# A state-space scan whose preparation moves into its own loop, with work shifted from VectorE to GpSimd and one transpose moved in the attention

## The reference, cut to what matters

```python
A = -jnp.exp(A_log)                                   # 512 x 16
xp = jnp.einsum('bld,rd->blr', x, x_proj_w)           # 48 rows: dt_in, B, C
dt = jax.nn.softplus(jnp.einsum('blr,dr->bld', dt_in, dt_proj_w) + dt_proj_b)
dA = jnp.exp(dt[..., None] * A)
dBx = dt[..., None] * B[:, :, None, :] * x[..., None]
def step(h, inp):                                     # over the 512 tokens
    dA_t, dBx_t, C_t = inp
    h = dA_t * h + dBx_t
    y = jnp.einsum('bdn,bn->bd', h, C_t)
    return (h, y)
y = jnp.moveaxis(ys, 0, 1) + D * x
```

## Time and profile before

| | us |
|---|---|
| median of 3 runs | 2287.24 |
| lowest, highest | 2269.8, 2289.48 |
| profiled execution, its own time | 2282.19 |
| its span, first to last instruction | 2280.4 |

### The profile page before, as it was taken

One profiled execution on the slowest core, in us unless ns is written; L12 is line 12 of the kernel. 1 busy time (PEld: TensorE's weight loads), 2 busy tenths in 40 slices (PEclk: granted clock), 3 DMA queues, 4 the chain that ended last, 5 costly groups with the idle time before them and its releaser, 6 DMA issues. The chain is left out here.

```text
span 2280.4 us, 27810 instructions
## 1 busy us (share of the span) xinstructions
PE 1827.1 (80%) x8232; PEld 1115.2 (49%) x8232; DVE 1625.2 (71%) x2905; ACT 804.5 (35%) x1301; POOL 736.5 (32%) x582
## 2 busy tenths in 40 slices
PE   6287778787758899936986888888873999999998
PEld 1022222222436888825862333333452777877786
DVE  4699999999634566665207888888458766667668
ACT  5243434343211444421213666666523111111112
POOL 2676767674250566654001000000011422112100
PEclk7599999999779898857996999999985999999999
DMA  8011111111030888753544333333000000000002
GB/s 300 23 42 38 37 37 37 37 37 32 13 148 6 280 282 277 247 166 134 193 187 112 85 91 88 84 94 80 3 30 28 28 28 28 1 28 28 1 1 74
DMA packets 102032, 197.64 MB, mean 87 GB/s; under 512 B 17257, under 2 KB 34025, under 8 KB 101019
## 3 DMA queue, kind: packets, MB, share of 16 engines
q1 hardware_dynamic: 96795, 179.46, 24.2%
q0 software_dynamic: 5120, 16.78, 2.2%
HBM read 130.72 MB, written 63.05 MB: 85 GB/s over the span
## 5 line engine op out<-in xcount | busy, mean ns | idle before, releaser
L1527 DVE TENSOR_REDUCE att_top<-att_first 128x1 f32<-128x512 f32 x512 | 332.4, 686 | 121.6 <-PE att_first L1407 111.6
L421 PE MATMUL scan_y<-scan_hc,all_ident 128*128 128x512 f32 x512 | 294.7, 663 | 101.8 <-DVE scan_hc L381 101.7
L355 POOL TENSOR_TENSOR scan_dbx<-ssm_U,scan_bbc 128x512 f32<-128x512 f32 x256 | 316.0, 1268 | 135.1 <-DVE scan_h L390 101.4
L390 DVE TENSOR_TENSOR_SCAN scan_h<-scan_da,scan_dbx 128x512 f32<-128x512 f32 x256 | 318.3, 1244 | 23.0 <-POOL scan_dbx L355 22.1
L1489 ACT ACTIVATE att_prob<-att_second 128x1024 f32<-128x1024 f32 x256 | 247.9, 1022 | 132.6 <-PE att_second L1427 130.6
L366 ACT ACTIVATE scan_da<-ssm_DT,ssm_A 128x512 f32 x256 | 176.8, 691 | 270.9 <-DVE scan_h L390 270.9
L421 PEld LDWEIGHTS scan_y<-scan_hc,all_ident 128*128 128x128 f32 x512 | 79.1, 194 | 314.0 <-DVE scan_hc L381 312.5
L1673 POOL TENSOR_TENSOR pairs_raw<-pairs_raw,pairs_scales 128x512 f32<-128x512 f32 x42 | 42.6, 1048 | 547.5 <-DMA pairs_raw<-in_w 547.5
L1803 ACT ACTIVATE ffn_silu<-ffn_pg 128x256 f32<-128x256 f32 x112 | 43.2, 386 | 415.2 <-PE ffn_pg L130 415.2
L128 PE MATMUL ffn_pg<-pairs_wh,last_XH 128*128 128x512 f32 x448 | 180.4, 403 | 1.7 <-PEq L431 1.7
L1407 PE MATMUL att_first<-att_ks,att_qs 48*128 48x512 f32 x512 | 133.8, 513 | 59.5 <-DVE att_top L1527 48.5
(11 more groups left out here) (272 smaller groups left out, 3913.7 us busy)
## 6 DMA issues: line engine op xcount, KB each, us to landing
mlps_raw<-in_w SPq DMA_DIRECT2D x26, 769.0 KB, 5.8
exp_raw<-in_w SPq DMA_DIRECT2D x24, 769.0 KB, 6.1
scan_bbc<-brow_dram SPq DMA_DIRECT2D x64, 256.0 KB, 3.1
sorted_x<-pre_zero SPq DMA_DIRECT2D x4, 3072.0 KB, 14.6
exp_x<-sorted_x SPq DMA_DIRECT2D x48, 256.0 KB, 4.2
sorted_y<-exp_y SPq DMA_DIRECT2D x48, 256.0 KB, 3.5
att_qs<-qk_dram SPq DMA_DIRECT2D x192, 64.0 KB, 2.2
att_ks<-qk_dram SPq DMA_DIRECT2D x192, 64.0 KB, 2.2
```

The lines of the kernel that those rows point to most:

```text
L355: nc.gpsimd.tensor_tensor(dbx[:, i % (2 * KC), :], g.U[:, c, bass.ts(b, NB)], bbc[:, n % RING, :], ALU.mult).then_inc(dbx_ready, 1)
L390: nc.vector.tensor_tensor_scan(h[:, i % HRING, :], da[:, i % 2, :], dbx[:, i % (2 * KC), :], 0.0, ALU.mult, ALU.add).then_inc(h_ready, 1)
L421: mm = pe.matmul(y[:, c, :], g.ident[:], hc[:, i % 2, :], start=(m == 0), stop=(m == STATE - 1))
L1527: nc.vector.tensor_reduce(top[w % 2][:, qt, item:item + 1], p_first[first_place(m) % FIRSTS][:], AX.X, ALU.max).then_inc(max_done, 1)
```

## The change: what it does

`ssm_inputs` and `ssm_scan` become one function, `ssm`, written out without loops. Batch 0 is prepared first and alone. Every later batch b + 1 is prepared while batch b is scanned: its instructions are put into fixed steps m (0 to 15) of that scan, between the scan's own. Per batch they are, on PE: `project_rows` in step 0, `project_z` in steps 2 to 5, `sum_dt` (four matmuls with the identity that add the four parts of softplus) in steps 11 to 14; on ACT: `copy_rows` and `copy_c` in step 1, `magnitude` and `positive` in steps 2 to 5, three sets of four in steps 6, 7 and 8, `logarithm` in step 9, `copy_dt` in steps 11 to 14; on POOL: `mask` and `masked_ln` in steps 10 and 11, `scaled_x` in steps 12 to 15. All of them share one PSUM buffer, `aux`.

In the scan, POOL makes `dbx` of all four chunks in one instruction of 2048 elements. In 12 of a batch's 16 steps (`pooled`) it also multiplies chunk 3's h by C (`weigh_last`, tile `hp`), with a C row that a DMA spreads; DVE keeps the other 52 of 64 products. C's row is split into two fp32r parts and spread by two fp32r matmuls (`spread`) into `cbc`, of which there is now one buffer. The four clearing DMAs are now issued together, after batch 0's rows are stored. In the attention `turn_max` moves from the end of step `kt == 0` to the middle of step `kt == 1`, behind `weigh` and ahead of the second pair of `first`.

```diff
-def ssm_inputs(nc, a, g):
+def ssm(nc, a, g):
 
...
+        def pooled(n):
+
+            return n % STATE not in (9, 10, 11, 13)
...
+            def store_rows(b):
+                sp.wait_ge(rows_copied, b + 1)
+                sp.dma_start(g.brow_dram[:, b, :], rows[AT_B, b % 2, :]).then_inc(stored[b % 2], 16)
+                sp.dma_start(g.crow_dram[:, b, :], rows[AT_C, b % 2, :]).then_inc(stored[b % 2], 16)
+
+            store_rows(0)
             for b in range(BATCH):
 
                 at = g.sorted_x.rearrange("(t p) d -> p t d", p=P)[:, b * CLEARS:(b + 1) * CLEARS, :]
                 sp.dma_start(at, zero[:].unsqueeze(1).to_broadcast([P, CLEARS, DIM])).then_inc(cleared, 16)
...
+            def inputs(n):
+                pool.wait_ge(b_in[n % RING], 16 * (n // RING + 1))
+                if n % STATE == 0:
+                    pool.wait_ge(u_ready, KC * (n // STATE + 1))
+                if n >= 2:
+
+                    pool.wait_ge(h_ready, KC * (n - 1))
+                nc.gpsimd.tensor_tensor(dbx[:, n % 2], u[:, n // STATE % 2],
+                                        bbc[:, n % RING, :].unsqueeze(1).to_broadcast([P, KC, NB]),
+                                        ALU.mult).then_inc(dbx_ready, 1)
+
+            def weigh_last(n):
+                k = by_pool(n)
+                pool.wait_ge(c_in[k % RING], 16 * (k // RING + 1))
+                pool.wait_ge(h_ready, KC * (n + 1))
+                if k >= 2:
+
+                    pool.wait_ge(y_pool, k - 1)
+                nc.gpsimd.tensor_tensor(hp[:, k % 2, :], cbs[:, k % RING, :], h[:, n % 2, LAST, :],
+                                        ALU.mult).then_inc(hp_ready, 1)
+
+            for c in range(KC):
+                mask(0, c)
+                masked_ln(0, c)
+            for c in range(KC):
+                scaled_x(0, c)
+            for n in range(STEPS):
+                b, m = n // STATE, n % STATE
+                inputs(n)
+                if n >= 2 and pooled(n - 2):
+                    weigh_last(n - 2)
+                if b + 1 < BATCH:
+                    if m in (10, 11):
+                        for c in range(2 * (m - 10), 2 * (m - 10) + 2):
+                            mask(b + 1, c)
+                            masked_ln(b + 1, c)
+                    if m >= 12:
+                        scaled_x(b + 1, m - 12)
+            weigh_last(STEPS - 2)
+            weigh_last(STEPS - 1)
...
+            def copy_rows(b):
+                act.wait_ge(rows_ready, b + 1)
+                if b >= 2:
+
+                    act.wait_ge(stored[b % 2], 32 * (b // 2))
+                    act.wait_ge(z_ready, KC * (b - 1))
+                nc.scalar.activation(rows[:, b % 2, :], aux[0:ROWS, :], ACT.Copy).then_inc(rows_copied, 1)
+
...
+            def magnitude(b, c):
+                act.wait_ge(z_ready, KC * b + c + 1)
+                if b:
+
+                    act.wait_ge(dt_summed, KC * b)
+                nc.scalar.activation(mag[:, c, :], z_of(b, c), ACT.Abs, bias=dtb[:, c:c + 1]).then_inc(mag_ready, 1)
+
+            def positive(b, c):
+                nc.scalar.activation(pos[:, c, :], z_of(b, c), ACT.Relu, bias=dtb[:, c:c + 1]).then_inc(pos_ready, 1)
+
...
+            def copy_dt(b, c):
+                act.wait_ge(dt_summed, KC * b + c + 1)
+                if b >= 2:
+
+                    act.wait_ge(da_ready, KC * STATE * (b - 1))
+                    act.wait_ge(u_ready, KC * (b - 1))
+                nc.scalar.activation(dt[:, b % 2, c, :], dt_sum(b, c), ACT.Copy).then_inc(dt_ready, 1)
...
+            for i in range(STEPS * KC):
+                n, c = i // KC, i % KC
+                b, m = n // STATE, n % STATE
+                if i >= 2:
+
+                    act.wait_ge(h_ready, i - 1)
+                if i == 0:
+                    act.wait_ge(a_ready, 2)
+                if m == 0:
+                    act.wait_ge(dt_ready, KC * b + c + 1)
+                nc.scalar.activation(da[:, i % 2, :], dt[:, b % 2, c, :], ACT.Exp,
+                                     scale=minus_a[:, c, m:m + 1]).then_inc(da_ready, 1)
+                if b + 1 < BATCH:
+                    if m == 1 and c == 0:
+                        copy_rows(b + 1)
+                    if m == 1 and c == 1:
+                        copy_c(b + 1)
+                    if 2 <= m < 2 + KC and c == 1:
+                        magnitude(b + 1, m - 2)
+                    if 2 <= m < 2 + KC and c == 2:
+                        positive(b + 1, m - 2)
+                    if m == 6:
+                        exponential(b + 1, c)
+                    if m == 7:
+                        one(b + 1, c)
+                    if m == 8:
+                        negative_rest(b + 1, c)
+                    if m == 9 and c == 0:
+                        logarithm(b + 1)
+                    if 11 <= m < 11 + KC and c == 3:
+                        copy_dt(b + 1, m - 11)
...
+            def weigh(n, c):
+                k = by_dve(n) + c
+                dve.wait_ge(h_ready, KC * n + c + 1)
+                dve.wait_ge(c_ready, n + 1)
+                if k >= 2:
+
+                    dve.wait_ge(y_own, k - 1)
+                nc.vector.tensor_tensor(hc[:, k % 2, :], cbc[:], h[:, n % 2, c, :], ALU.mult).then_inc(hc_ready, 1)
+
...
+            for n in range(STEPS):
+                for c in range(KC):
+                    i = n * KC + c
+                    dve.wait_ge(da_ready, i + 1)
+                    if c == 0:
+                        dve.wait_ge(dbx_ready, n + 1)
+                    if n >= 2:
+
+                        if c < LAST or not pooled(n - 2):
+                            dve.wait_ge(hc_ready, by_dve(n - 2) + c + 1)
+                        else:
+                            dve.wait_ge(hp_ready, by_pool(n - 1))
+                    nc.vector.tensor_tensor_scan(h[:, n % 2, c, :], da[:, i % 2, :], dbx[:, n % 2, c, :], 0.0,
                                                  ALU.mult, ALU.add).then_inc(h_ready, 1)
-                    if i:
-                        weigh(b, i - 1)
-                weigh(b, STEPS - 1)
-                for c in range(KC):
-
-                    dve.wait_ge(y_used_hc, b * STEPS + STEPS - KC + c + 1 + y_used_0)
-                    xs = g.XT[:, c, bass.ts(b, NB)]
-                    nc.vector.scalar_tensor_tensor(out=xs, in0=xs, scalar=g.D1[:, c:c + 1], in1=y[:, c, :],
-                                                   op0=ALU.mult, op1=ALU.add).then_inc(y_read, 1)
+                    if c:
+                        weigh(n, c - 1)
+                    elif n and not pooled(n - 1):
+                        weigh(n - 1, LAST)
+                    if n % STATE == 1 and c == 3 and n + STATE < STEPS:
+                        low_c(n // STATE + 1)
+                    if n >= STATE and n % STATE == 0 and c:
+                        sums(n // STATE - 1, c - 1)
+                    if n >= STATE and n % STATE == 2 and c == 0:
+                        sums(n // STATE - 1, LAST)
+            for c in range(KC):
...
+            def project_z(b, c):
+                pe.wait_ge(rows_copied, b + 1)
+                if b:
+
+                    pe.wait_ge(c_lo_ready, b + 1)
+                    pe.wait_ge(pos_ready, KC * b + c)
+                out = y[:, c, :] if b == 0 else aux[:]
+                pe.matmul(out, wdt[:, c * P:(c + 1) * P], rows[0:RANK, b % 2, :], start=True, stop=True).then_inc(z_ready, 1)
+
+            def sum_dt(b, c):
+                pe.wait_ge(pos_ready, KC * (b + 1))
+                pe.wait_ge(masked, KC * b + c + 1)
+                out = y[:, c, :] if b == 0 else aux[:]
+                if b:
+
+                    pe.wait_ge(dt_ready, KC * b + c)
+                for k, part in enumerate((mag, nrest, ln, pos)):
+                    mm = pe.matmul(out, g.ident[:], part[:, c, :], start=(k == 0), stop=(k == 3))
+                mm.then_inc(dt_summed, 1)
+
+            def spread(n):
+                b = n // STATE
+                if n % STATE == 0:
+                    pe.wait_ge(c_lo_ready, b + 1)
+                if n:
+
+                    pe.wait_ge(hc_ready, by_dve(n))
+                pe.matmul(cbc[:], sel[AT_C, n % STATE, :], c_hi[AT_C, b % 2, :], start=True, stop=False)
+                pe.matmul(cbc[:], sel[AT_C, n % STATE, :], c_lo[AT_C, b % 2, :], start=False, stop=True).then_inc(c_ready, 1)
+
...
+            for n in range(STEPS):
+                b, m = n // STATE, n % STATE
+                for c in range(LAST):
+                    if c == LAST - 1:
+                        ahead = n + 1 < STEPS and pooled(n)
+                        if ahead:
+                            spread(n + 1)
+                    gather(n, c)
+                    if n >= 2 and c == 0 and pooled(n - 2):
+                        gather(n - 2, LAST)
+                    if b + 1 < BATCH:
                         if m == 0:
-
-                            pe.wait_ge(y_read, b * KC + c + 1)
```

(20 more changed lines are left out.)

364 lines of the change are left out of this document (170 added, 194 removed).

## The result

The changed kernel takes 2321.14 us (median of 4 runs, 2317.3 to 2326.5) against 2288.36 for the kernel before in the same rounds: a ratio of 1.017, 95% interval 1.013 to 1.021. It is slower by 33 us; the forecast was 2313. The profiled execution of the changed kernel has a span of 2321.5 us, 41.1 more than before's 2280.4.

The account below looks back on a forecast made before the run. DVE was taken as the scan's bound, with 105.9 us of preparation ahead of 457.0 us of scan. From the profiled 2282.2 us: -45 (start), -33 (DVE), +128 (ACT's queue), -19 (attention) gave 2313 us, range 2240 to 2370.

Parts of the forecast that it names:

- The start: Ahead of the scan: with only batch 0 prepared first, the first scan comes at about 61 us, -45 us (-35 to -46).
- DVE's own work: In the scan: DVE's instructions take 424 us in place of 457.0, -33 us (-28 to -36).
- ACT's queue: In the scan: inserted ACT instructions that wait hold up the next exponentials, +128 us (113 to 200).
- steps 2 to 5: magnitude waits for project_z; DVE idles 4.6 us at full clock, 7.2 at low, twelve times: +71 us.
- step 9: The logarithm and its table loads between two exponentials idle DVE 2.9 us, three times: +9 us.
- steps 10 to 14: copy_dt waits for sum_dt in steps 11 to 14, at full clock: +38 us (86 at low clock).
- step 1: copy_rows waits for the last quarter of project_rows and delays the next exponentials: +10.5 us.
- rival (c): In the scan: POOL becomes the bounding engine, +4 us, 2317 without other waits; chance 0.05 of over 10 us.
- The attention: In the attention: moved transposes no longer wait for an exponential, 0.6 us per set in 31 sets, -19 us.
- Rival (a): In the scan: the inserted work is all hidden, 2185 us, chance 0.13; half the waits, near 2245, another 0.12.
- Rival (b): PE falls to the low clock in the whole stage: 2395 us, or 2350 to 2370 if partly; chance 0.15.
- The table load: At ACT's logarithm: no extra drain per switch; the skill's 1.38 us would add 8 us over six switches.

Follow-up runs that it names:

- warm: The changed kernel with four dummy PE matmuls adding zeros behind project_z in steps 2 to 5 of batches 0 to 2: 2312.1 us, ratio 1.014.
- z_early: The changed kernel with project_z ahead of the step's first addition on PE, magnitude and positive one exponential later on ACT: 2256.7 us, ratio 0.989.
- rows_late: The changed kernel with only copy_rows and copy_c moved behind chunks 2 and 3 of step 1 on ACT: ratio 1.018, stage 559.2 us.
- act_mask: all_early with sum_dt's matmuls cut in two pairs and the masks of batches 1 to 3 formed on ACT: 2209.9 us, ratio 0.973.
- turn_only: The kernel before with only the attention's edit, turn_max moved into step kt 1: 2264.4 us, ratio 0.990.
- all_early: The changed kernel with project_z and sum_dt earlier on PE, magnitude, positive, copy_rows and copy_c later on ACT: 2221.8 us, ratio 0.973.

## Why the prediction was right

The time, the sign and the places of the waits came out. In steps' lengths, the difference of the two spans is 41.1 us (forecast 31, from 50 - 19). That the sum is only 10 us off is in part luck: its third term was 24 us too small, and the start, DVE's work and the time behind the stage together came out 13.5 us lower than forecast.

- **The start**: -48.4 us, forecast -45. The logarithm ended at 30.3 instead of the 34.7 that I had, and the masks took back part of it, since POOL needs 1.92 us for one, three times the 0.62 that I took as half a product. Yet they hide under PE's sum of dt, 16.82 us from 33.92, of which some 5.7 us ran at the low clock (forecast 6):

```profile
30.50 1.93 POOL L256 TENSOR_SCALAR ssm_mask<-all_X 128x512 f32<-128x512 f32 x1 [24.30 <-ACT all_X L360]
...
33.92 16.82 PE L513 MATMUL ssm_y<-all_X,all_ident 128*128 128x512 f32 x32 [15.81 <-POOL all_X L261]
```

- **DVE's own work**: 573.1 less 151.6 of waits is 421.5 us, forecast 424.
- **ACT's queue**: steps 2 to 5 lose 75.1 us (forecast 71), step 9 loses 8.0 (9), steps 10 to 14 lose 47.7 (38), step 1 loses 20.8 (10.5). 151.6 us in all against 128, inside the range of 113 to 200. The recorded waits, 143.6 us for ACT and 2.2 for PE's additions, are lower, in part since they count from the end of the instruction before, which a row puts some 0.1 us after the next one could start. The largest term is right within 6%, and warm and z_early show its parts: 4.43 us a step at full clock (4.6 in the loop), and some 70 of the 75 us gone with the order. The first mis-sized term is step 1: the sum took PE to be level with DVE and at full clock. The windows of the kernel after at the end of step 0 and in step 1 show neither:

```profile
212.00:216.00 4.00, 4.00 (x6) 1.34 (x5) 4.00 (x6) 0.69 (x1) 2.85 (x3) 0.50 0.18 60
216.00:219.00 3.00, 3.00 (x7) 1.08 (x6) 1.24 (x2) 0.00 (x0) 3.00 (x1) 0.81 0.40 106
219.00:222.00 3.00, 3.00 (x8) 0.93 (x7) 0.00 (x0) 0.00 (x0) 1.76 (x2) 1.00 0.04 14
```

  PE is busy for 10 of 10 us, the first four at the low clock (0.50), with additions, `project_rows` and a spreading pair, which takes 0.66 us from start to start (218.74 to 219.40) where the term had 0.44; DVE has nothing left to do in the last 3, while `copy_rows` waits. rows_late shows 13.9 of the 20.8 us to be ACT's queue. The second is steps 10 to 14, by 10 us. Step 10, which no term had, takes 7.5 to 8.2 us instead of 6.85 (2.7 us in all). POOL's late `dbx` adds 4.1 us in step 11, since the sum had a mask at 0.62 us and it takes 1.92. And the full clock that this term took was not there all the time: step 12 of batches 1 and 2 takes 10.88 us, 1.5 more than in batch 0 and in warm, with a granted clock of 0.63 from 329 to 332, and in step 14 `hp`'s addition ahead of `sum_dt` takes 1.91 us instead of 1.02, at 0.63 from 351.0 to 354.6. The prediction's rival (c), POOL as the bound, is small but real: 4 us in the changed kernel, 12 in the mended order, where act_mask takes them away.
- **The attention**: a set takes 12.32 us instead of 12.92, some -19 us in 31 sets, forecast -19; turn_only bears it out by itself. The time behind the stage fell by 26.6 us. The other 8 are less than that time varies by: it lies between 1674 and 1707 us in the thirteen profiles that have the moved transposes.
- **Rival (a)**, all hidden, at 2185 or 0.955 of before, did not happen, but the change's idea was sound: with the order of the queues mended the same parts come to 2222 us (0.973 of before), and with the masks on ACT to 2197 to 2210 (0.969 to 0.973). The rival's number was not reached: all_early's steps still lose some 45 us. Its point was 3.2 us per wait; the waits measured 151.6 / 30 = 5.1. **Rival (b)** was half true: the clock did fall to 0.63 in steps 2 to 5, and was higher between them, but not always 1.00 (0.87 in steps 6 to 8). It cost some 22 us in steps 2 to 5 by warm's sum.
- **The table load**: the logarithm starts 0.02 us after its table has loaded (298.01 + 1.28 to 299.31), and the step loses 2.67 us, so the further 1.38 us per switch that the Trainium skill ("ScalarE: Activation LUTs", section What ACT_TABLE_LOAD costs) gives don't show here either.

## What to carry to other kernels

An idle engine is no room for work if the idle time lies before the very event that the inserted work waits for. Follow the inserted instruction round its loop: who produces its operand, what stands ahead of that in the producer's queue, and what stands behind the reader; then put the producer ahead of the loop's event and the reader behind the instructions that are due next. In a ring of two buffers a wait of 5 us in such a loop is paid in full at each step, and the same parts in another order (all_early against the changed kernel) took 105 us less in the stage, 468.0 instead of 573.1. And don't take the engine that the profile names for a wait on several as the last one: look up when each of them was done.

## What the runs showed of the hardware

- On POOL a `tensor_scalar` of 128 x 512 with multiply and minimum takes 1.93 us, longer than a product of two tensors (1.26 to 1.28 us). ACT's two activations for the same mask take 0.61 each and disappear.
- PE's granted clock was 0.63 and 0.68 in two steps in which PE was idle for 3 and 6 of 13 us. Four harmless matmuls (zeros added to a sum) in the idle time brought 1.00 and 0.97 back (two windows of warm) and paid for themselves: a stage 20.4 us shorter for some 41 us of added matmuls (12 x 3.4).
- PE to ACT to DVE took 1.16 us from a matmul at full clock to its reader (81.87 to 83.03) and 0.72 us from the exponential to the scan (83.61 to 84.33), less than the 0.96 of the earlier trace rows.
